# A routed cross-attention block: one softmax sum moved from ScalarE's accumulator to VectorE, and the first slots re-ordered

## The reference

```python
q = layernorm(x) @ Wq + bq                      # 16 heads of 16 features
k, v = ctx @ Wkv + bkv
attn = softmax(q @ k.T / 4)                     # per head, 128 x 128
x = x + (attn @ v) @ Wo + bo
# routed feed-forward
y = layernorm(x)
chosen = top 96 of the 128 rows of each sequence by y @ w_router
out = x + y, but x + gelu(y @ w_block) in the chosen rows
```

## Time and profile before

| | |
|---|---|
| median of 3 runs | 903.54 us |
| the profiled execution | 904.1 us |
| its span, first to last instruction | 902.3 us |
| mean granted clock of TensorE | 0.991 of full speed |
| busy share PE / DVE / ACT / POOL | 96% / 95% / 96% / 88% |

### The profile page before, as it was taken

How to read it: one execution, slowest core, us unless ns; L and a number is a source line. 1 busy time by engine, 2 the same in 40 slices (tenths; PEclk the granted TensorE clock), 3 DMA queues, 4 the chain that set the end, 5 groups by cost and what they waited for, 6 DMA issues and landing times. The chain is left out here.

```text
span 902.3 us, 30174 instructions
## 1 busy us (share of the span) xinstructions
PE 864.8 (96%) x9842; PEld 718.8 (80%) x9842; DVE 857.9 (95%) x2068; ACT 870.6 (96%) x4632; POOL 789.6 (88%) x1489
## 2 busy tenths in 40 slices
PE   6999999999999999999999999999999999999972
PEld 6778888888888888888888888888888888888752
DVE  5888999999999999999999999999999999999987
ACT  4999999999999999999999999999999999999984
POOL 5468879999999999999999999999999999998865
PEclk9999999999999999999999999999999999999997
DMA  7221123232323232223333222323222323211102
GB/s 233 69 65 53 54 63 86 79 93 59 84 82 89 72 96 69 79 79 85 84 83 91 57 80 88 91 72 95 61 85 79 87 78 90 75 40 40 41 24 94
DMA packets 71357, 70.40 MB, mean 78 GB/s; under 512 B 12064, under 2 KB 63520, under 8 KB 71200
## 3 DMA queue, kind: packets, MB, share of 16 engines
q1 hardware_dynamic: 69840, 67.68, 26.4%
q10 hardware_dynamic: 1360, 0.79, 0.3%
HBM read 35.13 MB, written 16.78 MB: 58 GB/s over the span
## 5 line engine op out<-in xcount | busy, mean ns | idle before, releaser
L646 ACT ACTIVATE e_sb<-ps_s,neg_max 128x128 f32<-128x128 f32 x2048 | 772.1, 639 | 2.8 <-DVE neg_max L805 2.7
L646 ACT ACTIVATION_READ_ACCUMULATOR e_sb<-ps_s,neg_max 128x1 f32 x2048 | 718.2, 464 | 0.0
L805 DVE TENSOR_REDUCE neg_max<-ps_s 128x4 f32<-128x512 f32 x512 | 331.0, 666 | 19.7 <-PE ps_s L385 18.2
L385 PE MATMUL ps_s<-q_eo,k_sb 32*128 32x256 f32 x2048 | 146.6, 399 | 3.6 <-ACT e_sb L646 1.5
L450 PE MATMUL ps_a<-e_sb,v_pad 128*32 128x128 f32 x4096 | 138.4, 276 | 1.5 <-POOL v_pad L1168 0.9
L344 PE MATMUL ps_a<-w_o_sb,o_sb 128*128 128x256 f32 x512 | 131.7, 379 | 4.0 <-DVE v_sb L929 3.8
L450 PEld LDWEIGHTS ps_a<-e_sb,v_pad 128*32 128x32 f32 x4096 | 104.1, 109 | 23.2 <-issue 21.5
L385 PEld LDWEIGHTS ps_s<-q_eo,k_sb 32*128 32x128 f32 x2048 | 95.8, 184 | 32.9 <-issue 28.7
L344 PEld LDWEIGHTS ps_a<-w_o_sb,o_sb 128*128 128x128 f32 x512 | 93.8, 189 | 22.8 <-issue 4.7
L1157 POOL TENSOR_TENSOR x_sb<-x_sb,bo_sb 128x256 f32<-128x256 f32 x128 | 105.1, 822 | 0.2
L1168 POOL TENSOR_TENSOR v_pad<-v_sb,recip 128x256 f32<-128x256 f32 x128 | 79.5, 621 | 29.1 <-DVE recip L865 27.1
(11 more groups left out here) (113 smaller groups left out, 2213.8 us busy)
## 6 DMA issues: line engine op xcount, KB each, us to landing
x_sb<-in_x SPq DMA_DIRECT2D x64, 256.0 KB, 3.0
c_sb<-in_ctx SPq DMA_DIRECT2D x64, 256.0 KB, 3.0
out<-z_sb SPq DMA_DIRECT2D x64, 256.0 KB, 2.4
q_eo<-q_raw SPq DMA_DIRECT2D x504, 32.0 KB, 2.0
z_sb<-in_L_xattn_Wkv ACTq DMA_DIRECT2D x2, 256.0 KB, 6.7
z_sb<-in_L_xattn_Wq ACTq DMA_DIRECT2D x1, 256.0 KB, 3.6
w_z_sb<-in_L_ffn_w_block SPq DMA_DIRECT2D x1, 256.0 KB, 8.0
w_o_sb<-in_L_xattn_Wo SPq DMA_DIRECT2D x1, 256.0 KB, 7.1
```

What stands on the lines that cost most here:

```text
L385: mm = nc.tensor.matmul(ps_s[:, bank(b, j), c, :, :], k_sb[rows, r2, c, h * T:(h + 1) * T], q_eo[rows, r2, :, c, h, :], start=True, stop=True)
L646: last = nc.scalar.activation(e_sb[:, b % 3, j, c, par, :], ps_s[:, bank(b, j), c, par, :], ACT.Exp, bias=neg_max[:, b % 4, h:h + 1], accu ...
L805: nc.vector.tensor_reduce(neg_max[:, b % 4, :].rearrange("p (c j q) -> p j c q", c=C, j=J)[:, j, :, :], ps_s[:, bank(b, j), :, :, :], AX.X ...
```

## The change

1. The last of the four exponentials of row group 1 (half 1, parity 1) loses its accumulator. Its sum is taken by a new VectorE step, `last_sum_of_group_1(b)`, a `tensor_reduce` of 128x1 from the 128x128 that the exponential wrote to SBUF. The step stands at the end of a slot, behind `product_scaled`, and `inverse_sums_01` waits for it as well.
2. In slot 2, TensorE's `queries_or_keys_of_pair(6, 0)` moves from ahead of `attention(1)` to behind it. VectorE's queue isn't changed there.
3. On SyncE's queue the copies of pair 2 move ahead of the loads of c of 8 and x of 14, the copies of pair 4 ahead of the load of c of 12, and x of 16 ahead of c of 14.
4. The second memset of `q_eo` on GpSimd moves from the opening to behind `input_and_bias(1)`.

```diff
@@ sync
             load_x(10)
             load_x(12)
+            queries_even_odd_of_pair(2)
+            load_c(8)
             load_x(14)
-            load_c(8)
             load_c(10)
-            queries_even_odd_of_pair(2)
+            queries_even_odd_of_pair(4)
             load_c(12)
+            load_x(16)
             load_c(14)
-            queries_even_odd_of_pair(4)
-            load_x(16)
             queries_even_odd_of_pair(6)
@@ tensor
                 if s < 4:
                     transpose_inputs(2 * s + 5)
-                if s == 2:
-                    queries_or_keys_of_pair(6, 0)
...
                 attention(s - 1, sure)
+                if s == 2:
+                    queries_or_keys_of_pair(6, 0)
@@ scalar, exps
                                                     accum_out=(ps_s[:, j, c, par, 0:1] if j >= 2 else
+                                                               None if (j, c, par) == (1, C - 1, 1) else
                                                                sums[:, b % 4, c, j, par:par + 1]))
@@ vector
+            def last_sum_of_group_1(b):
+
+                if has(b):
+                    dve.wait_ge(exp_ready[1], upto(b))
+                    nc.vector.tensor_reduce(sums[:, b % 4, C - 1, 1, 1:2], e_sb[:, b % 3, 1, C - 1, 1, :], AX.X,
+                                            ALU.add).then_inc(last_sum_ready, 1)
...
             def inverse_sums_01(b):
                 if has(b):
                     dve.wait_ge(exp_ready[0], upto(b))
+                    dve.wait_ge(last_sum_ready, upto(b))
...
             centre_block_weights()
+            last_sum_of_group_1(0)
             inverse_sums_01(0)
...
             inputs_low(7)
+            last_sum_of_group_1(1)
             stats1_of_pair(10)
...
                 product_scaled(s - 4, sure)
+                last_sum_of_group_1(s)
@@ gpsimd
             nc.gpsimd.memset(q_eo[:, 0, :, :, 2:4, :], 0.0).then_inc(q_eo_zero, 1)
-            nc.gpsimd.memset(q_eo[:, 1, :, :, :, :], 0.0).then_inc(q_eo_zero, 1)
...
             input_and_bias(1)
+            nc.gpsimd.memset(q_eo[:, 1, :, :, :, :], 0.0).then_inc(q_eo_zero, 1)
             rstd1_of_pair(6)
```

More of the change, by code:

```diff
@@ L193, in cross_attention_routed_ffn @@
         exp_ready = [sem(f"exp_ready{j}") for j in range(J)]
+        last_sum_ready = sem("last_sum_ready")
         recip_ready, recip_23_ready = sem("recip_ready"), sem("recip_23_ready")
```

## The result

The changed kernel takes 912.55 us (median of 4 runs, 911.9 to 913.11). The kernel before took 903.76 on the same chip. The ratio is 1.0094, with a 95% interval of 1.0082 to 1.0106: slower by 8.8 us. The forecast was 911.2. The profiled execution of the changed kernel has a span of 911.3 us, 9.0 above the one before.

A forecast was written before the change was run, and what follows sets the result against it. ScalarE was taken as the bound, with VectorE to become it. Terms 7.8 - 0.5 - 0.8 + 1.0 + 0.2 = +7.7 us gave 911.8 against the profiled 904.1, 911.2 for the median; range 902 to 915.

The forecast's parts named there:

- TensorE's pace: Rival, chance 0.17: VectorE takes the sum in without delaying TensorE; a group of eight slots takes 53.04 us, the kernel 897.9.
- The exponential: ScalarE, each slot: without accumulator it frees 0.12 us (bounds 0.09 and 0.21), so the slot falls from 6.69 to 6.57.
- that rival: Rival, chance 0.05: the program keeps the accumulator read, ScalarE frees nothing, and the kernel takes 912.5 us.
- The reduce: VectorE, each slot: the new sum is a step of 0.20 us, with bounds of 0.16 and 0.29.
- The groups: Twelve groups of eight slots, 155.09 to 797.12: VectorE becomes the bound, 54.15 us each instead of 53.50, +7.8; chance 0.62.
- The budget: VectorE, eight slots: 1.60 us of new work against 0.95 of room, so 0.65 don't fit.
- count by slots: VectorE needs 6.82 us in five router slots, 6.46 in three others; said to give 54.15 for a group too.
- Early slots: The eight slots from 74.62 to 128.02: VectorE's new work fits, ScalarE is the only bound there, -0.5 us.
- Last ten slots and tail: The last ten full slots, 797.12 to 861.55: ScalarE's saving shortens them, -0.8 us.
- Queries of pair 6: Slot 3: its scores wait for inverse_sums_23(2), queued on VectorE behind queries_of_pair(6), whose queries now end later: +1.0 us.
- first sum: last_sum_of_group_1(0) on VectorE stands on the path to the scores of slot 2: +0.2 us.
- SyncE and the memset: The opening: SyncE's new order of copies and loads and GpSimd's moved memset change nothing, 0 us.

The follow-up runs named there:

- relief_no_sum: The kernel before, with the last exponential of row group 1 without accumulator and nobody making its sum (1.0 in its place): 900.66 us, ratio 0.999.
- order_only: The kernel before with only SyncE's new order of loads and copies and GpSimd's memset moved behind input_and_bias(1): 903.83 us, ratio 1.0005.
- sum_no_relief: The kernel before with all accumulators kept and VectorE making the same sum once more into a spare tile: 912.14 us, ratio 1.0112.
- sum_32: The kernel before with that exponential's accumulator dropped and VectorE summing only 32 of the 128 elements: 905.1 us, ratio 1.0033.
- pair6_only: The kernel before with only TensorE's queries of pair 6 moved behind attention(1): 905.03 us, ratio 1.0011.

## Why the prediction was right, and where its working was not

**What bounds the kernel.** ScalarE's slot at 6.69 and VectorE as the next bound: right. "At most 0.66 us in a group, 8 us in all" for ScalarE's relief: too high by far as a bound. relief_no_sum gains 0.02 in a group against the earlier trace rows and 0.14 against order_only, which ran on another chip than relief_no_sum. The prediction took VectorE's waits in three slots as room for all eight. It was visible: in the earlier trace rows a router slot takes VectorE 6.62 from maxima to maxima, with no wait, already above TensorE's 6.58, and the same trace has two in each group that take 6.86 and 6.94. VectorE's 33.73 for five router slots and TensorE's 3 x 6.58 = 19.74 for the others are 53.47, which is what relief_no_sum measured (53.48), not 53.04. So the rival "TensorE's pace" was given a time that no price of the reduce could reach in these groups.

**The exponential.** 0.09 instead of 0.12. It changes little, since the relief counts only outside the groups. The Trainium skill's page "ScalarE: Activation LUTs", section "What ACT_TABLE_LOAD costs", has figures from which the prediction worked out a step of 0.294 and a relief of 0.05; the trace has a step of 0.25 and a relief of 0.09, and that decides. The accumulator read is gone, 1920 reads instead of 2048: that rival is false.

**The reduce.** Price 0.20, measured 0.19 to 0.20 (433.24 to 433.43 in the trace; 269 ns for one against 285 in the earlier trace rows). This price was read from another shape and it carried the forecast: with 0.16 it would have been 3.8 us less.

**The groups.** +7.8 forecast; +9.6 against the trace it was worked out from, +8.1 against order_only. The mechanism "VectorE becomes the bound" is shown by sum_no_relief, by sum_32 and by the idle times. The budget of 8 x 0.20 - 0.95 was right to 0.15, but by the wrong count: sum_32, where the budget says nothing, cost 0.30 over relief_no_sum. The count that fits is that of the router slots alone: 1.02 more than without a sum (five steps, and 0.12 of `final` in one slot), less 0.19 that the first slot behind them gives back. The prediction had a count by slots beside the budget and wrote that the two give the same. They don't, with its own numbers: 5 x 6.82 + 3 x 6.46 is 53.48, not 54.15, because it took 6.62 for every router slot. That the budget came near the result is in part luck.

**Outside.** Early slots -0.5 forecast, -0.7 measured. Last ten slots and tail -0.8 forecast, +0.35 measured, the one term with the wrong sign: seven of these ten slots (116 to 120, 124, 125) have router steps, so that stretch is no window of ScalarE's alone. It takes 64.32, against 64.43 before; relief_no_sum needs 64.21 there, sum_no_relief 64.94. Slot 126 costs 0.19 or 0.20 more in every kernel with the whole sum in every slot.

**The start.** Queries of pair 6 +1.0 forecast, 1.20 measured (1.21 in pair6_only), by the chain that was named; first sum +0.2, measured 0.26; SyncE and the memset 0, measured 0 within 0.15%. Not forecast: the traced start of before had TensorE at its low clock.

**The hit on the time.** From trace to trace the groups came out 1.8 above their term and the end 1.15 above, and the 1.6 by which the first scores came earlier, mostly the low clock of before, took more than half of that back: 9.0 in the span, where 10.6 would stand without it, against 7.7. Part of the hit is owed to that. How far it holds for the median of 912.55 isn't known, as it isn't known which executions of before had the low clock; sum_no_relief, on the second chip, was 10.0 above the kernel before there.

**The signs.** ScalarE's idle time rose to 0.80 in a group and VectorE's fell: as said. VectorE's waits for the scores became shorter but did not go (0.09 and 0.19 are left of 0.31 and 0.45). TensorE's transposes wait longer for the product in three of five router slots and in the slot behind them; the waits for the reciprocal and for `residual` weren't named. The scores of slot 3 weren't near 41.6, for the start's reason, but 1.20 late. The reduce's row is 269 ns.

## What to carry to other kernels

Room on an engine is worth something only in the slots where it stands: compare each slot's own chain with the pace of the others, and add the excess up slot by slot, before trusting a budget over a period. Test "engine X is the bound" by giving X its relief with nothing in exchange; here that showed a second bound right below the first (53.48 us in a group against 53.50). When work is moved in the queue of one engine, look at what is queued on the other engines behind the wait for it; moving that too may only hand the wait to the next slot.

## What the runs showed of the hardware

- The read of an accumulator in SBUF costs ScalarE 0.09 us of its queue (steps of 0.34 before and 0.25 after); the exponential's own step of 0.25 is as long as that of the cast of twice its size.
- A VectorE reduce to 128x1 has a step of 0.20 for 128 elements and 0.10 for 32 (269 and 169 ns in after and sum_32), so 96 elements cost 0.10.
- The early eight slots take 53.40 us in two traces and 53.55 in two others where ScalarE is the bound, and 52.72 or 52.73 in all ten where TensorE is; chip and execution aren't told apart.
- TensorE's clock was at 1.2 GHz from 12 to 15 us in one trace of fourteen. It had idled 1.13 us behind its first transposes; four others had idled 1.15 to 1.30 there and were at 2.4.
- `final`, which reads two SBUF tensors, takes from 0.42 to 0.72 us, and the length goes with where GpSimd's steps stand beside it (0.42 where one starts 0.06 behind it, at 442.11 before; 0.55 where one starts 0.26 behind it, at 438.70 after).
